# Key updates of a gated scan moved from VectorE to GpSimd, its score blocks copied by ScalarE, and wider matmuls in five scan levels

## The reference, cut to what matters

```
c = qkva as complex numbers; q, k, v, a = c[..., 0..3]      # 8 heads of 32 channels
a = a * (rsqrt(|a|^2) * sigmoid(log(|a|^2)))                # the gate, one number per position and channel
kv = einsum('blhd,blhe->blhde', k, v);  kv[:, 0] += a[:, 0] * h0
h[t] = a[t] * h[t-1] + kv[t]                                # an associative scan over the positions
y = einsum('blhd,blhde->blhe', q, h)
```

## Time and profile before

| | before |
|---|---|
| median of 3 runs | 3893.76 us |
| profiled execution, its own time | 3925.24 us |
| its span, first to last instruction | 3923.4 us |
| PE busy | 2883.7 us (73%) |
| DVE busy | 2113.1 us (54%) |
| ACT busy | 928.3 us (24%) |
| POOL busy | 652.6 us (17%) |
| mean granted TensorE clock | 0.780 |

### The profile page before, as it was taken

How to read it: one execution, slowest core, us unless ns; L and a number is a source line. 1 busy time by engine, 2 the same in 40 slices (tenths; PEclk the granted TensorE clock), 3 DMA queues, 4 the chain that set the end, 5 groups by cost and what they waited for, 6 DMA issues and landing times.

```text
span 3923.4 us, 112483 instructions
## 1 busy us (share of the span) xinstructions
PE 2883.7 (73%) x51136; PEld 2151.2 (55%) x51136; DVE 2113.1 (54%) x4928; ACT 928.3 (24%) x1820; POOL 652.6 (17%) x682
## 2 busy tenths in 40 slices
PE   4268669867885898488749875986678466999990
PEld 3254357435743674466447545743564346888880
DVE  4446766576658556856685577658543841000004
ACT  0212133113311431142223213311321131222220
POOL 0314200410060006002500330042000000000006
PEclk8578767867786878587858776886769578999995
DMA  2122201210021122012201220121011005555545
GB/s 78 22 55 49 45 3 50 65 30 33 30 66 20 40 39 59 10 39 50 49 9 40 60 45 4 44 65 32 9 46 41 4 15 189 198 195 191 197 156 174
DMA packets 230141, 249.52 MB, mean 64 GB/s; under 512 B 147360, under 2 KB 187168, under 8 KB 227360
## 3 DMA queue, kind: packets, MB, share of 16 engines
q1 hardware_dynamic: 223520, 225.54, 20.1%
q0 software_dynamic: 6144, 16.79, 1.4%
HBM read 196.15 MB, written 46.14 MB: 62 GB/s over the span
## 4 chain that ended last, share of the span: by engine, by line
PE 63%; issue 14%; DVE 8%; POOL 5%; ACT 4%; DMA 1%; SPq 0%; POOLq 0%; DVEq 0%
PE bank L1780 13%; PE bank L2075 10%; PE bank L2278 7%; PE bank L2297 7%; PE bank L2013 4%; POOL arena L1672 3%; PE bank L2090 2%; PE bank L2095 2%; PE bank L1790 2%; PE bank L1907 2%; POOL arena L1716 2%; PE bank L1912 2%; PE bank L1917 1%; PE bank L2035 1%; PE bank L1886 1%
## 5 line engine op out<-in xcount | busy, mean ns | idle before, releaser
L1672 POOL TENSOR_TENSOR arena<-arena 128x1 f32<-128x1 f32 (+30 forms) x496 | 435.1, 907 | 639.4 <-DMA arena<-n_d 467.9
L2075 PE MATMUL bank<-arena 32*32 32x32 f32 (+1 forms) x13824 | 205.6, 253 | 232.2 <-issue 226.0
L2075 PE MATMUL bank<-arena,xn 32*32 32x32 f32 (+1 forms) x13824 | 203.4, 258 | 226.2 <-issue 226.2
L1693 POOL DMA_INDIRECT h_d<-h_tok,pos_now x64 | 66.2, 1035 | 1753.5 <-DVE pos_now L1537 1736.5
L1128 DVE TENSOR_REDUCE arena<-arena 128x1 f32<-128x1 f32 (+30 forms) x496 | 243.7, 502 | 173.3 <-POOL arena L1672 168.9
L1780 PE MATMUL bank<-hT,ring 128*128 128x512 f32 x640 | 316.1, 647 | 8.2 <-DVE arena L1272 8.2
L2075 PEld LDWEIGHTS bank<-arena 32*32 32x32 f32 x13824 | 181.8, 134 | 254.3 <-issue 241.2
L2075 PEld LDWEIGHTS bank<-arena,xn 32*32 32x32 f32 x13824 | 179.3, 135 | 242.6 <-issue 242.1
L2278 PE MATMUL bank<-arena 128*128 128x256 f32 x1248 | 276.6, 380 | 0.0
L2297 PE MATMUL bank<-arena 128*128 128x256 f32 x1248 | 275.6, 379 | 0.0
L2278 PEld LDWEIGHTS bank<-arena 128*128 128x128 f32 x1248 | 237.7, 191 | 32.8 <-issue 0.4
(11 more groups left out here) (332 smaller groups left out, 5185.8 us busy)
## 6 DMA issues: line engine op xcount, KB each, us to landing
arena<-in_w_ring SPq DMA_DIRECT2D x78, 1024.0 KB, 5.0
ring<-in_w_ring SPq DMA_DIRECT2D x104, 512.0 KB, 4.9
arena<-h_d SPq DMA_DIRECT2D x39, 256.0 KB, 5.3
y_d<-arena SPq DMA_DIRECT2D x39, 256.0 KB, 5.8
n_d<-NA SPq DMA_DIRECT2D x8, 1024.0 KB, 3.9
arena<-n_d SPq DMA_DIRECT2D x16, 512.0 KB, 8.1
u_d<-arena SPq DMA_DIRECT2D x8, 1024.0 KB, 3.8
NA<-u_d SPq DMA_DIRECT2D x32, 256.0 KB, 5.9
```

Of the source, the lines that this page charges most:

```text
L1672: pool.tensor_tensor(part, Usub[:, c, 0:t, 0:t], Nsub[:, c, t, 0:t].unsqueeze(1).to_broadcast([P, t, t]), ALU.mult)\
L2075: i_ = mm(bank[4 * hg + h][keys, b * width:(b + 1) * width], K2[rows_, r, b, keys], q, start=(r == 0), stop=(r == 1), skip_group_check=True)
```

## The change

1. Steps k = 1 to 5 use tiles of 32 rows and 128 columns: for each batch and plane, 4 matmuls (one per head) of all 128 keys against the 64 query positions in later halves (two planes, 128 columns). There were 16 of 32 keys against 32 columns. The results of a head fill its whole bank, and only blocks on the diagonal of 32 by 32 are of use.
2. The 8 banks are one PSUM tensor, so that one instruction can read the four heads of a group.
3. For steps 2 to 5, ACT copies the diagonal blocks from PSUM to a tile raws[hg] (take_blocks: 4 copies of 32 partitions and 512 elements), and DVE's predicated copy reads from there: one instruction of 512 elements per partition for all heads. For step 1, DVE copies straight from PSUM in 4 instructions of 32 partitions; for step 0 in one instruction of 1024 elements.
4. All key updates (partial products and sums, 7 levels, 2 groups) move to POOL, which gets turn_key_columns. The signal k_ready is POOL's now.
5. Waits follow: PE waits for block_ok where it waited for masked; ACT waits for scored and for the masked of the level before; DVE waits for block_ok; SP starts the load of X_next after a q_ready too.

```diff
-        bank = [ctx.enter_context(nc.psum_tensor(f"bank{i}", [P, 512], F32)) for i in range(8)]
+        banks_ = ctx.enter_context(nc.psum_tensor("banks", [P, 8, 512], F32))
+        bank = [banks_[:, i, :] for i in range(8)]
+        raws = [TTb[:, i] for i in range(HG)]
...
@@ ScalarE
+                    def take_blocks(k, hg):
+                        act.wait_ge(*at(scored, 2 * k + hg + 1))
+                        if k > 2:
+                            act.wait_ge(*at(masked, 2 * (k - 1) + hg + 1))
+                        half = BLK // 2
+                        for n in range(NCH):
+                            blk = slice(BLK * n, BLK * n + BLK)
+                            ins_ = act.activation(
+                                raws[hg][blk].rearrange("p (h g t) -> p h g t", h=HP, t=half),
+                                banks_[blk, 4 * hg:4 * hg + HP, :].rearrange("p h (g c) -> p h g c", g=2 * B)
+                                [:, :, :, half * n:half * n + half], ACT.Copy)
+                        ins_.then_inc(*up(block_ok, me))
...
+                    act.wait_ge(*at(q_ready, 3 * HG))
+                    act.wait_ge(*at(k_ready, HG))
+                    for k, hg in itertools.product(range(2, INNER + 1), range(HG)):
+                        take_blocks(k, hg)
@@ VectorE, take_scores
-                        for h in range(HP):
-                            ... (one predicated copy per head, from its bank)
+                        if k == 0:
+                            dve.copy_predicated(... 128 partitions, 1024 elements, from banks_)
+                        elif k == 1:
+                            for n in range(NCH):
+                                ins_ = dve.copy_predicated(... 32 partitions, 512 elements, from banks_)
+                        else:
+                            dve.wait_ge(*at(block_ok, 2 * (k - 2) + hg + 1))
+                            dve.copy_predicated(
+                                near_score.rearrange("p h b r (n two m) -> p (h b r) n two m", two=2, m=m)[:, :, :, 1],
+                                allow.unsqueeze(1).to_broadcast([P, HP * 2 * B, width // m, m]),
+                                raws[hg].rearrange("p (g n m) -> p g n m", n=width // m, m=m)).then_inc(*up(masked, me))
@@ VectorE, the loop over levels and groups
-                        dve.tensor_tensor(tmp(u1), kk, over(Ta[:, 0]), ALU.mult).then_inc(*up(dve_step, me))
-                        dve.tensor_tensor(tmp(u2), kk, over(Ta[:, 1]), ALU.mult).then_inc(*up(dve_step, me))
...
-                        dve.tensor_tensor(kk[:, 0], tmp(u1)[:, 0], tmp(u2)[:, 1], ALU.subtract)
-                        dve.tensor_tensor(kk[:, 1], tmp(u1)[:, 1], tmp(u2)[:, 0], ALU.add).then_inc(*up(k_ready, me))
@@ GpSimd
+                    def turn_key_columns(hg, lev):
+                        ...
+                        pool.wait_ge(*at(a_ok, 2 * lev + hg + 1))
+                        settle()
+                        pool.tensor_tensor(v1, kk, over(later[:, 0]), ALU.mult).then_inc(*up(key_part, me))
+                        pool.tensor_tensor(v2, kk, over(later[:, 1]), ALU.mult).then_inc(*up(key_part, me))
+                        settle()
+                        pool.wait_ge(*at(scored, 2 * (lev + 1) + hg + 1))
+                        pool.tensor_tensor(kk[:, 0], v1[:, 0], v2[:, 1], ALU.subtract)
+                        pool.tensor_tensor(kk[:, 1], v1[:, 1], v2[:, 0], ALU.add).then_inc(*up(k_ready, me))
+                    for lev, hg in itertools.product(range(LEVELS), range(HG)):
+                        turn_key_columns(hg, lev)
@@ TensorE, level
-                            if lev <= INNER:
-                                pe.wait_ge(*at(masked, HP * (2 * lev + hg + 1)))
+                            if lev < 2:
+                                pe.wait_ge(*at(masked, 2 * lev + hg + 1))
+                            elif lev <= INNER:
+                                pe.wait_ge(*at(block_ok, 2 * (lev - 2) + hg + 1))
...
-                                for x in range(HP * NCH if lev < INNER else 2 * HP if lev == INNER else HP):
+                                for x in range(HP * NCH if k == 0 else 2 * HP if lev == INNER else HP):
...
+                                    elif lev < INNER:
+                                        keys = slice(0, SEG)
+                                        q = q.rearrange("p r (n two m) -> p r n two m", two=2, m=1 << lev)[:, :, :, 1]
+                                        width = SEG
```

More of the change, by code:

```diff
@@ L329, in build @@
         u_in = signal("u_in", nxt=64)
-        dve_step = signal("dve_step", rest=226, nxt=13, pre=36)
+        dve_step = signal("dve_step", rest=198, nxt=13, pre=36)
         pre_var = signal("pre_var", pre=1)
@@ L358, in build @@
         q_ready = signal("q_ready", rest=18)
-        masked = signal("masked", rest=48)
+        masked = signal("masked", rest=12)
+        block_ok = signal("block_ok", rest=8)
         state_ok = signal("state_ok", rest=2)
@@ L434, in build @@
         k_ready = signal("k_ready", rest=14)
+        key_part = signal("key_part", rest=28)
         numbered = signal("numbered")
@@ L1339, in take_scores @@
                         allow = near_masks[:, a:a + width].bitcast(I32).rearrange("p (n m) -> p n m", m=m)
[L1340 to L1344 removed]
+                        if k == 0:
                             dve.copy_predicated(
[L1346 to L1347 removed]
+                                near_score.rearrange("p h b r t -> p h (b r) t"),
+                                near_masks[:, 0:BLK].bitcast(I32).unsqueeze(1).unsqueeze(1).to_broadcast([P, HP, 2 * B, BLK]),
+                                banks_[:, 4 * hg:4 * hg + HP, 0:2 * B * BLK].rearrange("p h (g t) -> p h g t", g=2 * B))\
@@ L1552, in turn @@
                              q_ready, masked, state_ok, hsq_ok, rt_var, rt_gap, hot_ok,
-                             pos_ok, k_ready])
+                             pos_ok])
                 dve.sem_inc(started.handle, 1)
@@ L1686, in turn, with over @@
                         pool.memset(pair.rearrange("p h b r t -> p h (b r t)"), 0.0).then_inc(*up(zeroed, me))
+                    def turn_key_columns(hg, lev):
+                        m = 1 << lev
+                        w = level_table(hg, lev).rearrange("p r (j two) -> p r j two", two=2)
+                        later = w[:, :, :, 1]
+                        kk = K2s[hg][:, :, :, :].rearrange("p r b (n two m) -> p r (b n) two m", two=2, m=m)[:, :, :, 0]
+                        def over(v):
+                            return v.unsqueeze(1).unsqueeze(3).to_broadcast([P, 2, NT // (2 * m), m])
+                        v1, v2 = [u[:, :, 0:NT // 2].rearrange("p r (n m) -> p r n m", m=m) for u in (u1, u2)]
+                        if lev == 0:
+                            pool.wait_ge(*at(plane_ok, 6 * hg + 6))
+                            pool.wait_ge(*at(a_ok, hg + 1))
+                        else:
+                            pool.wait_ge(*at(a_ok, 2 * lev + hg + 1))
[8 more added lines that the diff above has]
+                        turn_key_columns(hg, lev)
                     settle()
@@ L1700, in turn @@
                     settle()
-                counted(seg, [zeroed, sub_mul])
+                counted(seg, [zeroed, sub_mul, key_part, k_ready])
                 pool.sem_inc(started.handle, 1)
```

24 lines of the change are left out of this document (14 added, 10 removed).

## The result

The changed kernel took 3911.77 us (median of five runs, 3907.19 to 3914.08); the kernel before took 3893.76 in five runs beside it. The ratio is 1.0043, 95% interval 1.0029 to 1.0058: 18 us slower. The forecast was 50 us slower. The direction was right, the size was not. Timed again on another chip, with the kernel before beside it, the same kernel came out at 1.0078 (1.0057 to 1.0098), 30 us slower.

The account below looks back on a forecast made before the run. PE's instruction supply and DVE were both taken to bind the scan steps; adding DVE's and POOL's times gave 95.8 us a segment against 89.6, eight times 6.2 or 50 us over 3893.8: 3944 us, own range 3880 to 4010.

Parts of the forecast that it names:

- What bounds the kernel: Scan steps: PE's instruction supply, 7.5 us per step and group, and DVE's nearly equal timeline both bind; 89.6 us a segment.
- PE's wider tiles: Steps 1 to 5 on PE: 64 records in 3.7 us, 7.4 for a pair of groups against 15 before.
- The row-tile rival: 32x128 tiles don't run four at a time on PE: a step takes 8.2 us, 4000 us in all; chance 0.05.
- DVE's part: DVE in the levels: loses 2.0 us of key work per iteration; step 1's copies cost 3.1 us a group.
- The exclusion: Levels of the scan: DVE and POOL instructions reading SBUF shut each other out, so both engines' times add.
- The first two rivals: Scan: no exclusion, 3694 us, chance 0.14; or DVE waits for POOL but POOL never for DVE, 3758 us, chance 0.12.
- POOL's operands are not dear: Rival denied here: POOL a fifth slower on strided and broadcast operands, 9.4 us a segment more, 4019 us; chance 0.12.
- The sum: Up to group 0's outputs: DVE and POOL times added, with smaller terms, to 95.8 us a segment against 89.6.
- some 2: Overlap at each change of turn between DVE and POOL, 0.55 instead of 0.69 us, gives back some 2 us a segment.
- The end: End of the stretch: PE's step 7 of group 0 must follow the shared DVE and POOL work, 3.7 us.
- sum of 95.8: First level instruction to first output matmul in a segment: 95.8 us against 89.6, 6.2 us longer.
- the 88 that would have made the forecast wrong: Sign to check: group 0's outputs starting under 88 us after the first level instruction would refute the forecast; some 96 expected.

Follow-up runs that it names:

- both together: Changed kernel with the key updates back on DVE and step 1 back in 32x32 tiles with one 128-partition predicated copy; ratio 0.9748 to the kernel before.
- the doubled products: Changed kernel with POOL's two key products of every level done twice, same results; ratio 1.0463 to the kernel before, 4060 us.
- A clearing on POOL: Changed kernel with POOL's four key instructions replaced by clearings of about their length that read nothing, keys not updated; ratio 0.9629 to the kernel before.

## Why the prediction was right or wrong

*What bounds the kernel.* Right that the supply of instructions binds, wrong that "both bind: taking work from one alone gives little". DVE's own work was 62 of the 74.3 us; the 12.18 busy of 15 in the earlier trace rows already left room. Taking the key work from DVE alone, a third of its work, left near at 73.6, as was said. Taking PE's records alone (both together) brought it to 61.8, 2.5% of the time. The change gained this on PE and gave it back with step 1's copies and with POOL.

*PE's wider tiles.* Right. At the granted clock of 0.50, 64 records in 3.7 us were said:
```profile
871.00 3.80 PE L2135 MATMUL banks<-arena,xn 32*128 32x128 f32 x64 [6.54 <-DVE arena L1466]
877.16 3.48 PE L2135 MATMUL banks<-arena 32*128 32x128 f32 x64 [2.36 <-DVE arena L1466]
```
With a mean granted clock of 0.75 it is 2.66 (834.34 in the same timeline). The row-tile rival is out.

*DVE's part.* The copies of steps 2 to 5, alone, are 1.3 us at step 2 (taken: 1.0) and 0.70 above (0.65), 6.8 in all for 5.9. Step 1's four copies were taken at 3.1 us a group and cost 5.19, just outside their bounds of 2.4 to 5.1: 32 partitions cost 1.29 us each, as much as 128. I put the two groups at 6.2 us, half of it lent to POOL; they are 10.4.

*The exclusion.* Right as a mechanism. The first two rivals are out: without the exclusion of two-input instructions near would be 53.9, not 76.8; and POOL waits too: its four groups of products have means of 1.31 to 1.58 us where 1.29 is the undisturbed row above. POOL's operands are not dear: that undisturbed row, with the level 1 strides, has 1.29 against 1.27 taken. At the coarser levels it is cheaper: undisturbed, it takes 1.15, 1.09, 1.07 and 1.05 us at levels 2 to 5, and 1.05 at level 6 in the rows of the kernel before with its keys on POOL.

*The sum is the step that failed*: "So I add both engines' times instead of taking the longer", with "some 2" us given back for the change of turn. In the near part, by measured durations: queries 10 x 2.15, tables 10.2, copies 6.8 and 10.4, together 48.9 of DVE (with 20 of keys that makes 68.9, and 69.2 was measured with the keys on DVE); DVE never waits for PE in the near part (its 18.7 us of waits at line 1465 are one in each tail). Of the 76.8 us, 27.9 are left for POOL, and the keys put back on DVE give 27.6. POOL did 11 iterations there, 42.9 us of work at the 3.9 taken and some 39.6 by its undisturbed lengths (products 1.24 to 1.01 from start to start, sums 0.69): it cost 0.7 of its own time, and the doubled products 0.6. The missing 12 us are where POOL runs under the copies from PSUM, 5.6 us in the segment of the rows, and in the handovers, worth some 0.7 us in the four products shown above; how the rest splits was not measured.

By the prediction's own prices the near part is 21.5 + 10.2 + 5.9 + 3.1 for DVE, 42.9 + 1.3 for POOL, less 1.6 of the 2 for handovers: 83.3. POOL's part of it, 42.6, is 14.7 too long, some 3.3 of that by its price at the coarser levels and the rest by overlap that the sum left out; step 1 is 7.3 and steps 2 to 5 are 0.9 too short. That makes the 6.5 between 83.3 and 76.8. The forecast came as near as it did by luck: step 1's copies were priced too low by half of what POOL's share was priced too high.

*The end.* I let DVE and POOL share the path up to the outputs, 13 and 12 iterations, and 3.7 us behind them. The shared path ends with the last near copy, 10 and 11 iterations in; from there ScalarE's queue and step 7 are the chain for 14.5 us, before as after (DVE's update for the outputs is ready at 13.4 and 13.6). What was left for this part in the sum of 95.8 was 12.5, 2.0 too short. So outputs were said to start 95.8 us after the first level product and started at 91.3, over the 88 that would have made the forecast wrong: 36 us in eight segments. The 89.6 that I compared with, one segment's, is 0.8 above the mean of 88.8, which takes back 6. That leaves 20 us slower by the stretches, where the medians say 18.

*Small terms.* The doubt that DVE's predicated copy from raws is of the excluded kind was settled: its mean in the changed kernel is 1.14 and 1.75 us for the two groups, 0.86 with the keys on DVE. ACT's copies stayed hidden, as said.

## What to carry to other kernels

Work given to GpSimd that reads SBUF, beside VectorE work with two SBUF inputs, is neither parallel nor fully serial: here it cost 0.6 to 0.7 of its own time, more than the 20 us that it took off VectorE. It can be hidden where something else sets the pace, and the pace has to be checked for each stretch: in the kernel before the same move cost nothing in levels 0 to 4 and 1.4% once it ran on into levels 5 and 6. Before sharing a bound between two engines, look whether one of them stands waiting for the other: DVE's idle time, 12 of 74 us, said that PE's supply alone was worth taking away. When a wide matmul makes the copy behind it run on fewer partitions, price the copy by its elements per partition: one narrow step with one full-width copy was better than four copies of a quarter.

## What the runs showed of the hardware

*What excludes what.* A clearing on POOL left DVE's two-input products at 692 and 684 ns and its two-input predicated copies at 853, but held the one-input negation, 661 for 294 ns. The Trainium skill's page SBUF — State Buffer, section "SBUF: two separate sides", has two SBUF inputs count only against a GpSimd instruction that reads SBUF; the trace agrees.

*Predicated copies* go by elements per partition, not by partitions: 1.29 us for 32x512 and for 128x512 from PSUM with the finest stride. The stride counts as well: step 0's copy of 128x1024 neighbouring elements takes 1.29 too.

*The same kernel, 23 us apart outside the change.* In the repeated run, records of 32x32 tiles of the delta rule (line 1928; 1872 in the kernel before) came in single drops for 6 us where they had come in one flow. The group, first and second run of the changed kernel:
```profile
L1928 PE MATMUL banks<-arena 32*32 32x64 f32 x2048 | 59.7, 259 | 18.1 <-issue 13.6 <-ACT arena L774 4.3
```
```profile
L1928 PE MATMUL banks<-arena 32*32 32x64 f32 x2048 | 67.4, 285 | 24.4 <-issue 19.9 <-ACT arena L774 4.3
```
and in the second run one such place:
```profile
1061.69 0.32 PE L1932 MATMUL banks<-arena 32*32 32x64 f32 x4 [0.43 <-issue]
1062.43 0.21 PE L1932 MATMUL banks<-arena 32*32 32x64 f32 x1 [0.41 <-issue]
...
1063.93 0.21 PE L1928 MATMUL banks<-arena 32*32 32x64 f32 x1 [0.44 <-issue]
```
The profiled execution of the kernel before has the long form too (65.1, 277, with 22.8 until issue, at line 1872), and lies 31 us above its median. The kernel with the near keys on POOL, profiled on the same chip as the repeated run, has it as well (67.3, 282). What makes the instructions come so is open. A stretch read in the trace told the change to 0.1 us where ratios moved by 0.35% between chips.
